# Linear attention stage of a decoder: each gram issued in three pieces among projections, values and decay sums; output projections at the end of a group

## What is computed

```python
q = split(x @ Wq.T); k = split(x @ Wk.T); v = split(x @ Wv.T)          # 4 heads, 32 / 32 / 64 features
g = log_sigmoid(x @ Wgk1.T @ Wgk2.T + bgk2) / 32                        # per-channel log decay
# S_t = diag(exp(g_t)) S_{t-1} + k_t v_t^T ;  o_t = q_t^T S_t           # per head
o = o * rsqrt(mean(o * o) + eps) * rms_w
x = layernorm(x + (o * silu(x @ Wg.T)) @ Wout.T)
```

## Time and profile before

| | |
|---|---|
| median of 3 runs | 1534.83 us (1534.75 to 1535.68) |
| profiled execution | 1551.76 us, of it the profile's span 1549.8 us |
| busy in the span: PE, PEld | 1314.0 us (85%), 865.7 us (56%) |
| busy: DVE, ACT, POOL | 1214.9 us (78%), 1045.9 us (67%), 801.9 us (52%) |
| mean granted TensorE clock | 0.888 |
| linear attention, from the first copy of `xT` to its last matmul in the next stage | 13 to 486 us |

### The profile page before, as it was taken

One profiled execution on the slowest core, in us unless ns is written; L12 is line 12 of the kernel. 1 busy time (PEld: TensorE's weight loads), 2 busy tenths in 40 slices (PEclk: granted clock), 3 DMA queues, 4 the chain that ended last, 5 costly groups with the idle time before them and its releaser, 6 DMA issues.

```text
span 1549.8 us, 63521 instructions
## 1 busy us (share of the span) xinstructions
PE 1314.0 (85%) x26424; PEld 865.7 (56%) x26438; DVE 1214.9 (78%) x2629; ACT 1045.9 (67%) x2244; POOL 801.9 (52%) x1590
## 2 busy tenths in 40 slices
PE   4788889899876777776767779999999999999897
PEld 2455556566544444443333346667666666666685
DVE  2455757677556889887899969999999999999755
ACT  3455656677546778876666667777777777777545
POOL 2445546576555778776788843344333332332123
PEclk9788889999878889987575679999999999999878
DMA  7000000000000000000000000000000000000012
GB/s 196 16 2 3 2 3 3 3 4 3 2 9 16 17 23 18 24 10 17 1 1 1 1 1 3 3 3 3 3 3 10 24 17 17 24 17 10 2 42 69
DMA packets 28670, 24.27 MB, mean 16 GB/s; under 512 B 3676, under 2 KB 23906, under 8 KB 28386
## 3 DMA queue, kind: packets, MB, share of 16 engines
q1 hardware_dynamic: 28386, 20.21, 4.6%
HBM read 15.94 MB, written 4.19 MB: 13 GB/s over the span
## 4 chain that ended last, share of the span: by engine, by line
PE 42%; POOL 23%; issue 20%; DVE 7%; ACT 6%; SPq 0%; POOLq 0%; DMA 0%; another core or an unknown queue 0%; DVEq 0%; ACTq 0%
PE keys_T L590 7%; PE keys_O L571 5%; POOL gla_low L1156 4%; PE keys_O L577 4%; PE keys_E L485 3%; PE keys_S L331 3%; POOL gla_yg L1186 3%; POOL gla_gate L1179 2%; POOL cross_pairs L837 2%; PE keys_E L528 2%; ACT keys_pT L657 2%; POOL gla_sq L1173 2%; POOL cross_spread L804 2%; PE keys_O L597 2%; DVE ffn_hh L2009 2%
## 5 line engine op out<-in xcount | busy, mean ns | idle before, releaser
L340 POOL TENSOR_SCALAR keys_spread<-keys_kT,keys_heads 128x512 f32<-128x512 f32 x128 | 86.8, 695 | 231.2 <-ACT keys_kT L621 231.2
L657 ACT ACTIVATE keys_pT<-keys_T 128x512 f32<-128x512 f32 x256 | 152.4, 595 | 76.5 <-PE keys_T L590 73.1
L350 DVE TENSOR_REDUCE keys_mx<-keys_S 128x16 f32<-128x1024 f32 x128 | 156.2, 1220 | 16.7 <-PE keys_S L331 15.0
L590 PE MATMUL keys_T<-ident_sb,keys_pexp 128*128 128x128 f32 x1024 | 165.4, 284 | 3.2 <-ACT keys_pT L657 2.3
L353 DVE TENSOR_TENSOR keys_pe_in<-keys_S,keys_mx 128x1024 f32<-128x1024 f32 x128 | 156.7, 1224 | 4.4
L590 PEld LDWEIGHTS keys_T<-ident_sb,keys_pexp 128*128 128x128 f32 x1024 | 113.0, 141 | 72.8 <-ACT keys_pT L657 38.3
L673 ACT ACTIVATE keys_pexp<-keys_pe_in 128x1024 f32<-128x1024 f32 x128 | 134.7, 1053 | 0.0
L710 DVE RECIPROCAL keys_rinv<-keys_O 128x128 f32<-128x128 f32 x128 | 120.4, 941 | 0.1
L1631 DVE COPY_PREDICATED gla_at<-gla_node,gla_GP 128x256 f32<-128x256 int32 x128 | 65.2, 509 | 59.6 <-ACT gla_at L1483 56.3
L571 PEld LDWEIGHTS keys_O<-keys_pT,keys_vz 128*32 128x32 f32 x4096 | 63.1, 110 | 64.1 <-ACT keys_pT L657 63.7
L1156 POOL TENSOR_TENSOR gla_low<-gla_ex,gla_kT 128x128 f32<-128x128 f32 x160 | 71.9, 482 | 51.2 <-ACT gla_ex L1474 51.2
(11 more groups left out here) (286 smaller groups left out, 3773.1 us busy)
## 6 DMA issues: line engine op xcount, KB each, us to landing
context<-in_ctx_T SPq DMA_DIRECT2D x32, 256.0 KB, 2.6
xs<-in_x SPq DMA_DIRECT2D x8, 512.0 KB, 7.6
out_x<-xs SPq DMA_DIRECT2D x16, 256.0 KB, 2.3
keys_mask_q<-keys_mask_b SPq DMA_DIRECT2D x64, 1.0 KB
keys_bias_right_f<-in_alibi_right SPq DMA_DIRECT2D x1, 512.0 KB, 3.9
ffn_w<-in_L_ffn_w_gate_T SPq DMA_DIRECT2D x1, 256.0 KB, 4.6
ffn_w<-in_L_ffn_w_up_T SPq DMA_DIRECT2D x1, 256.0 KB, 4.8
ffn_w<-in_L_ffn_w_down_T SPq DMA_DIRECT2D x1, 256.0 KB, 5.2
```

What stands on the lines that cost most here:

```text
L350: nc.vector.tensor_reduce(m, quads(S), X, ALU.max).then_inc(c["mx"], 1)
L590: last = nc.tensor.transpose(T[:, j * P:(j + 1) * P], pexp[:, t % 2, (4 * half + j) * P:(4 * half + j + 1) * P], sh.ident[:, :])
L657: nc.scalar.activation(pT[:, t % 2, 4 * half:4 * half + 4, :].rearrange("q n k -> q (n k)"), T[:, :], ACT.Copy).then_inc(c["pT"], 1)
```

## The change

In TensorE's body each gram is called three times, with two levels each, and only the last call signals. `gram(g, 1)` is issued as levels 4 and 5 right after `mix(g, 0)`, levels 0 and 1 after `keys(g+1)`, levels 2 and 3 after the first values. `gram(g+1, 0)` is issued as levels 0 and 1, then `values 3`, levels 2 and 3, then `decay_sums 3`, then levels 4 and 5. `decay_sums 3` with its exponential on ScalarE moves from the start of the next body to the end of this one. The two output projections of group g-1 move from the start of body g+1 to the end of body g: one ahead of `mix(g, 1)`, one after `decay_sums 1`; the first residual on VectorE moves with them, and two outputs leave the drain. ScalarE copies `values 3` after `decays 2` instead of before. The bias matmul of line 480 is issued one body earlier.

```diff
--- before.py
+++ after.py
@@ -474,11 +474,12 @@
         @stage.on("tensor")
         def _(pe):
             def prepare(stage_, g):
-                if stage_ == 0 and g == 0:
+                if stage_ == 0 and g == -1:
                     pe.wait_ge(c["weights"], NW)
                     pe.wait_ge(c["prep"], 2)
                     nc.tensor.matmul(OB[1][:, 2 * P:2 * P + D], bv_all[:, :], wo[0][:, :], start=True, stop=True) \
                         .then_inc(c["bo"], 1)
+                if stage_ == 0 and g == 0:
                     pe.wait_ge(c["bo"], 2)
 
             def project(w, src, name):
@@ -1281,9 +1282,10 @@
                                             decay[rows, :], start=True, stop=True)
                 last.then_inc(c["ex_done"], 1)
 
-            def gram(g, p, i):
-                free_back(pe, "at", g, i, AT, 1)
-                for level in range(LEVELS):
+            def gram(g, p, i, levels, opens=False, closes=False):
+                if opens:
+                    free_back(pe, "at", g, i, AT, 1)
+                for level in levels:
                     if level < LEVELS - 2:
                         await_pair(pe, "up", g, i, level + 1, UP)
                     else:
@@ -1304,7 +1306,8 @@
                                     last = nc.tensor.matmul(GP[s_ * SEQ:(s_ + 1) * SEQ, col:col + SEQ + HALF],
                                                             kT[rows, p, key], qu[rows, p, seq, :],
                                                             start=True, stop=True)
-                last.then_inc(c["gram"], 1)
+                if closes:
+                    last.then_inc(c["gram"], 1)
 
             def mix(g, p, i):
                 await_pair(pe, "at", g, i, AT, AT)
@@ -1336,14 +1339,7 @@
                 last.then_inc(c["out_done"], 1)
 
             def body(g, p, ahead):
-                m, n, l, k = live(g), live(g + 1), live(g - 1), live(g - 2)
-                if k:
-                    output(g - 2, 0)
-                if m:
-                    c.await_nth(pe, "ex", g, 3, G)
-                    decay_sums(g, p, 3)
-                if k:
-                    output(g - 2, 1)
+                m, n, l = live(g), live(g + 1), live(g - 1)
                 if n:
                     turn_x(g + 1, 1 - p)
                 if l:
@@ -1360,16 +1356,20 @@
                 if m:
                     c.await_nth(pe, "vg", g, G, G)
                     mix(g, p, 0)
+                    gram(g, p, 1, (4, 5), opens=True)
                 ahead(1)
                 if n:
                     keys(g + 1, 1 - p)
                 if m:
-                    gram(g, p, 1)
+                    gram(g, p, 1, (0, 1))
                 ahead(2)
                 if n:
                     c.await_nth(pe, "g", g + 1, 1, 1)
                     c.await_nth(pe, "za", g + 1, 1, 1)
                     values_and_gates(g + 1, 1 - p, 0, EA)
+                if m:
+                    gram(g, p, 1, (2, 3), closes=True)
+                if n:
                     c.await_nth(pe, "kT", g + 1, 1, 1)
                     values_and_gates(g + 1, 1 - p, 1, EB)
                     c.await_nth(pe, "vg", g + 1, 1, G)
@@ -1386,6 +1386,8 @@
                     if l:
                         await_pair(pe, "yT", g - 1, 1, 1, 1)
                     decay_sums(g + 1, 1 - p, 0)
+                if l:
+                    output(g - 1, 0)
                 if m:
                     if n:
                         c.await_nth(pe, "vg", g + 1, 3, G)
@@ -1393,19 +1395,23 @@
                 if n:
                     c.await_nth(pe, "ex", g + 1, 1, G)
                     decay_sums(g + 1, 1 - p, 1)
+                if l:
+                    output(g - 1, 1)
+                if n:
+                    c.await_nth(pe, "ex", g + 1, 2, G)
+                    decay_sums(g + 1, 1 - p, 2)
+                    gram(g + 1, 1 - p, 0, (0, 1), opens=True)
                     if m:
                         await_pair(pe, "o", g, 1, 1, 1)
                     else:
                         c.await_nth(pe, "vg", g + 1, 3, G)
                     values_and_gates(g + 1, 1 - p, 3, OB)
-                    c.await_nth(pe, "ex", g + 1, 2, G)
-                    decay_sums(g + 1, 1 - p, 2)
-                    gram(g + 1, 1 - p, 0)
+                    gram(g + 1, 1 - p, 0, (2, 3))
+                    c.await_nth(pe, "ex", g + 1, 3, G)
+                    decay_sums(g + 1, 1 - p, 3)
+                    gram(g + 1, 1 - p, 0, (4, 5), closes=True)
 
             def drain(n):
-                if n == 0:
-                    output(NG - 2, 0)
-                    output(NG - 2, 1)
                 if n == 1:
                     await_pair(pe, "yT", NG - 2, 1, 1, 1)
                     turn(NG - 1, 0, EB)
@@ -1516,7 +1522,6 @@
                     gates(g, p, 0)
                     cross(g, 0)
                     gates(g, p, 1)
-                    decays(g, 3)
                     gates(g, p, 2)
                 if n:
                     inputs(g + 1, 1 - p)
@@ -1552,11 +1557,12 @@
                     outputs(g, p, 1)
                 if n:
                     decays(g + 1, 1)
-                    values_and_gates(g + 1, 1 - p, 3, OB)
                 if k:
                     normalise(g - 2, p, 3)
                 if n:
                     decays(g + 1, 2)
+                    values_and_gates(g + 1, 1 - p, 3, OB)
+                    decays(g + 1, 3)
 
             def drain(n):
                 if n == 0:
@@ -1699,8 +1705,6 @@
                     mean_square(g - 1, 1 - p)
                     refine_roots(g - 1)
                     scaled(g - 1, 1 - p, 0)
-                if k:
-                    residual(g - 2, p, 0)
                 if m:
                     place(g, p, 0)
                 if k:
@@ -1716,12 +1720,13 @@
                 if m:
                     place(g, p, 1)
                     sum_squares(g, p, 0)
+                if l:
+                    residual(g - 1, 1 - p, 0)
                 if n:
                     upper(g + 1, 1 - p, 0)
 
             def drain(n):
                 if n == 0:
-                    residual(NG - 2, 0, 0)
                     sum_squares(NG - 1, 1, 1)
                     mean_square(NG - 1, 1)
                     residual(NG - 2, 0, 1)
```

## The result

| | before | after |
|---|---|---|
| median, 6 runs each | 1536.06 us | 1550.77 us |
| lowest to highest | 1534.75 to 1545.34 us | 1547.98 to 1553.68 us |
| span of the profiled execution | 1549.8 us | 1547.5 us |
| last `xT` copy of the linear attention, profiled | 415.0 us | 429.2 us |

The ratio is 1.0074 with a 95% interval of 1.0042 to 1.0106: slower by 0.4 to 1.1%. The two profiled spans stand the other way round, and the stages say why. At the last `xT` copy of the linear attention after is 14.2 us behind; the hand-over gives 3.8 back, the following stages 2.0; and then the last sublayer, whose code the change doesn't touch, takes 72 us in the profiled execution of before and 61 in that of after, with 27 us at half clock in the one and 8 in the other.

A forecast was written before the change was run, and what follows sets the result against it. Bound: a group loop with a 22.3 us good state, losing first to issue waits. Thirteen 27.5 us periods +14.1, first group -3.6, remaining issue waits +2, hand-over -4: +8.5 added to the median, rounded up to 1544 us, range 1512 to 1574.

The forecast's parts named there:

- good state: Linear attention group period at full clock, 22.3 us with TensorE busy 21.3; the average group loses 4.5 us against it.
- issue waits: TensorE running dry at boundaries of 256 instructions passed too fast, mainly in grams; some 26 us in all.
- The sum of 3.2 us: At TensorE's boundaries, the time for the 256 instructions ahead and the wait behind them together make about 3.2 us.
- The pieces: TensorE's grams split among wide matmuls: issue waits keep 2 us of some 30; returns to wide matmuls cost 0.2 per group.
- ScalarE's chain: ScalarE's work from exponential 3 to `xT`, uncovered at a group's start: `gate_logits` at 11.25 us after `decay_sums 1`, before 9.1.
- The undisturbed period: Linear attention group where nothing disturbs it: 25.7 us, 3.3 over the good state.
- The clock's price: Half clock after TensorE's standstill before `gate_logits`: 1.8 us per group, making the period 27.5.
- The ends: First linear attention group 28.5 us instead of 32.1, -3.6; hand-over without outputs in the drain, about -4 us.
- The sum: Thirteen periods +14.1, first group -3.6, remaining issue waits +2, hand-over -4: +8.5, added to the median for 1544 us.
- The clock holds: Rival, chance 0.22: the clock returns at once or TensorE's standstill is shorter; periods 25 to 26.3, 1521 us.
- The issue waits stay: Rival, chance 0.08: waits come with the count of instructions, not their pace; 26 us return in place of 2, 1568 us.
- ScalarE's chain does not decide: Rival, chance 0.10: something placed too late in the group comes earlier; period 22.6, 1480 us.

The follow-up runs named there:

- the moved boundaries: Kernel before with 32 matmuls of 32 by 32, read by nobody, added at TensorE's start: 1521.9 us, ratio 0.986.
- six kernels above: Before, after, split grams only, moved outputs and decay_sums 3 only, before with 32 added matmuls (1521.9 us), and split grams with ScalarE's chain still covered (1500.2 us).
- the kernel with the filled pause: Changed kernel with four matmuls of 256 columns ahead of the first turn and one after it, read by nobody: 1530.8 us, ratio 0.993.
- the moves alone: Changed kernel with whole grams, outputs, residual and decay_sums 3 moved as in the change: 1564.6 us, ratio 1.013.
- the first: Changed kernel with ScalarE's inverse roots and gates 0 ahead of exponential 3 instead of behind it: 1535.6 us, ratio 0.994 against 1.007 of the changed kernel.
- the sixth experiment: Changed kernel with both output projections and the residual back ahead of turn_x: 1525.4 us, ratio 0.989 against 1.007 of the changed kernel.
- the pieces alone: Kernel before with the grams split and ScalarE's values 3 copy after decays 2; outputs and decay_sums 3 left in place: 1525.8 us, ratio 0.988.

## Why the prediction was right, point by point

- *What bounds the kernel.* The good state of 22.3 us and the issue waits as its main loss: borne out by the moved boundaries, which take the same groups from 28 to 22.3 us. That the pace of 256 instructions decides was worked out from one trace; the count over six kernels above bears it out. The sum of 3.2 us is a mean and no rule, though: in the kernel before the time of the 251 recorded instructions and the wait behind them add up to anything from 2.0 to 4.1 us, and there is a wait of 1.1 behind a stretch of 2.8, where the prediction has none. What brings the instructions in so late isn't shown; nothing here looks into the fetching itself.
- *The pieces.* Forecast: 18 us of issue waits in the grams to under 4. They are 1.4.
- *ScalarE's chain.* Forecast: exponential 3 at 5.5, `gate_logits` at 11.25 us after `decay_sums 1`. Measured 5.36 and 10.9. The pause was forecast at 3.8 us and is 3.4 (2.65 and 0.75).
- *The undisturbed period*, 25.7 us: 25.66 in the kernel with the filled pause. That it fits so well is partly luck: up to `gate_logits` it takes 10.9 us instead of 11.25, and the rest of the group 14.7 instead of 14.4.
- *The clock's price*, 1.8 us: 1.6 in the quiet groups (27.27 - 25.66). In the mean of thirteen groups it is 1.7. Its size was right, its spread was not: in six groups of the changed kernel the clock is down for about 6.8 us at a time instead of 3.4, and four of those periods are 28.3 to 29.1.
- *What the prediction left out.* It gives a period "where nothing disturbs it" and then takes it thirteen times. But not all thirteen are undisturbed: in one of them VectorE prepares weights of a later sublayer, which makes it 1.8 us longer, a term that the prediction put at nothing. With the clock up but for 3.4 us, the thirteen groups still took 340.2 us and not 13 x 25.7 = 334. In the changed kernel they take 362.7, where the prediction has 357.5 and 2 of issue waits: 3.2 us more.
- *The ends.* First group 27.4 us, forecast 28.5, was 32.1: 1.1 us better than forecast. The hand-over gave 3.8 us, forecast 4.
- *The sum.* Forecast +8.5 us up to the hand-over, 1544 us and a range of 1512 to 1574; the profiled linear attention shows +14.2 - 3.8 = +10.4, and the medians +14.7. In the linear attention the 3.2 us that the groups took too long and the 1.1 that the first one gained partly cancel, which is luck. The other 4 us lie between profiled and timed executions, of which I had noted that the trace can't tell it. Taking +8.5 over to a median of 1535 was a choice; the last sublayer's 27 us at half clock, which the profiled execution of before had and that of after had not (of the others, only that of the moves alone had as much), shows that the difference between them was partly outside the linear attention.
- *The rivals.* "The clock holds" is what the filled pause makes of the kernel. "The issue waits stay" fell with 1.4 us. The Trainium skill, in "Runtime: NRT & Kernel Launch", section "Instruction fetch mechanics", says that crossing a block of 256 instructions is mostly hidden. The traces here agree where the instructions come slowly (no wait over 0.3 us where 251 recorded ones took over 2.9 us), and differ where they come fast, in whole grams above all (0.4 to 2.4 us at every boundary where they took under 2.2 us). "ScalarE's chain does not decide" fell with the first and the sixth experiment.

## What to carry to other kernels

A good change and a bad one can come in one edit: here the pieces alone won 1.2%, and with the moves on top the kernel lost 0.7%. Before steps leave a place, ask what ran beside them on the other engines; a list that looks like three harmless steps of TensorE may be the cover of a chain on ScalarE. And when a wait is "issue" and comes back every so many instructions, count the instructions: where dense runs of tiny matmuls are broken up with wide ones, most of the wait goes, and where they can't be, a few dozen small matmuls at the start may move it. Last, count what other stages put into the loop: a group that also prepares the next stage's weights is not the quiet group that one has worked out.

## What the runs showed that I had not expected

- 32 small matmuls that nobody reads, put ahead of everything, made the kernel before 1.4% faster (0.986, 0.981 to 0.990). A change of a few instructions anywhere ahead of dense stretches can move a time by as much as a real improvement, and should be told apart from it.
- Work put into a pause made a kernel 1.5% faster, since the clock stayed up: TensorE's 2.5 us of useless matmuls per group returned 1.6 us.
- The changed kernel's quiet period is 27.26 or 27.27 us in seven groups, the last five of them running, while those of the kernel before scatter from 22.27 to 30.33 behind its first. Why it locks so exactly isn't shown.
